# A graph-attention and mixture-FFN kernel: the square of a pair's second tile of updated rows moves from the end of ScalarE's slot to its beginning

## The reference: what is computed

```
xn    = layernorm(x)                       # before: x + attention
Wh    = xn @ W.T ; e = leaky_relu(ei[:,None] + ej[None,:], 0.2)
alpha = softmax(where(adj == 0, -inf, e))  # 1024 x 1024 per graph
x1    = x + alpha @ Wh                     # "updated rows"
feat  = mean over the 16 graphs of layernorm(x1) ; w = softmax(feat @ Wr + br)
out   = x1 + sum over 8 experts of w * (three-layer FFN of layernorm(x1))
```

## Time and profile before

| | |
|---|---|
| median of 3 runs | 2808.72 us (2807.88 to 2809.81) |
| time of the profiled execution | 2809.31 us |
| its span in the profile | 2807.4 us |
| PE busy / PEld busy | 2774.5 us (99%) / 2469.6 us (88%) |
| DVE busy / ACT busy / POOL busy | 2413.1 (86%) / 2106.8 (75%) / 487.5 us (17%) |
| attention part | about 0 to 683 us, 128 slots |
| granted TensorE clock | 0.998 of full speed |

### The profile page before, as it was taken

One profiled execution on the slowest core, in us unless ns is written; L12 is line 12 of the kernel. 1 busy time (PEld: TensorE's weight loads), 2 busy tenths in 40 slices (PEclk: granted clock), 3 DMA queues, 4 the chain that ended last, 5 costly groups with the idle time before them and its releaser, 6 DMA issues.

```text
span 2807.4 us, 46140 instructions
## 1 busy us (share of the span) xinstructions
PE 2774.5 (99%) x17114; PEld 2469.6 (88%) x17114; DVE 2413.1 (86%) x3408; ACT 2106.8 (75%) x2832; POOL 487.5 (17%) x707
## 2 busy tenths in 40 slices
PE   8999999999999999999999999999999999999998
PEld 7999999998788888888888888888888888888887
DVE  8999999997888888888888888888888888888887
ACT  7889889887777777777777777777777777777775
POOL 4555555555000000000000000000000000001000
PEclk9999999999999999999999999999999999999999
DMA  4455555543455554545445455545545554545554
GB/s 163 154 167 163 157 166 162 162 153 119 139 170 165 161 166 154 165 156 161 163 155 165 154 165 161 165 153 170 157 163 157 160 164 154 166 154 163 153 162 145
DMA packets 160060, 445.91 MB, mean 159 GB/s; under 512 B 16032, under 2 KB 73800, under 8 KB 159840
## 3 DMA queue, kind: packets, MB, share of 16 engines
q1 hardware_dynamic: 159840, 442.98, 50.2%
HBM read 401.99 MB, written 40.93 MB: 158 GB/s over the span
## 4 chain that ended last, share of the span: by engine, by line
PE 74%; DVE 1%; ACT 0%; issue 0%; DMA 0%; DVEq 0%; ACTq 0%
PE head_ps L53 12%; PE head_ps L55 12%; PE head_ps L54 12%; PE m_ps L1284 7%; PE m_ps L1287 7%; PE m_ps L1286 7%; PE z_ps L55 4%; PE z_ps L53 4%; PE z_ps L54 4%; PE turn_ps L1257 1%; PE turn_ps L1265 1%; DVE h_lo L1569 0%; DVE h_sums L1576 0%; DMA wo_ops<-wo_scratch 0%; ACT h_hi L1432 0%
## 5 line engine op out<-in xcount | busy, mean ns | idle before, releaser
L1416 ACT ACTIVATE h<-head_ps,bn_shift,bn_scale 128x512 f32<-128x512 f32 x768 | 593.9, 774 | 532.5 <-PE head_ps L55 319.9
L1569 DVE TENSOR_TENSOR h_lo<-h_sums,h_hi 128x1792 fp32r<-128x1792 f32 (+1 forms) x257 | 518.2, 2017 | 199.9 <-ACT h_hi L1432 199.8
L1432 ACT ACTIVATE h_hi<-h_sums 128x1792 fp32r<-128x1792 f32 (+1 forms) x257 | 435.4, 1694 | 63.6 <-DVE h_sums L1589 58.0
L1576 DVE TENSOR_TENSOR h_sums<-h,gate_row 128x1024 f32<-128x1024 f32 x256 | 313.7, 1225 | 114.5 <-ACT h L1416 96.7
L87 POOL TENSOR_TENSOR ffn_vareps<-ffn_mv,ln_eps 128x4 f32<-128x4 f32 x32 | 7.1, 223 | 1860.4 <-DVE ffn_mv L81 1860.4
L1536 DVE TENSOR_TENSOR h_lo<-h,h_hi 128x1024 fp32r<-128x1024 f32 x256 | 311.9, 1218 | 6.8 <-ACT h_hi L1446 6.8
L53 PE MATMUL attn_ps<-wh_hi,pT_hi 128*128 128x256 f32 x1024 | 304.9, 298 | 0.0
L54 PE MATMUL attn_ps<-wh_lo,pT_hi 128*128 128x256 f32 x1024 | 287.9, 281 | 0.0
L55 PE MATMUL attn_ps<-wh_hi,pT_lo 128*128 128x256 f32 x1024 | 287.8, 281 | 0.0
L1446 ACT ACTIVATE h_hi<-h 128x1024 fp32r<-128x1024 f32 x256 | 270.9, 1058 | 0.1
L1284 PE MATMUL m_ps<-h_hi,wo_ops 128*128 128x256 f32 x896 | 256.0, 286 | 3.1 <-DMA wo_ops<-wo_scratch 3.1
(11 more groups left out here) (215 smaller groups left out, 7619.3 us busy)
## 6 DMA issues: line engine op xcount, KB each, us to landing
wh_lo<-wo_scratch SPq DMA_DIRECT2D x124, 896.0 KB, 6.4
wo_ops<-wo_scratch SPq DMA_DIRECT2D x124, 896.0 KB, 6.5
adj_sb<-in_adj SPq DMA_DIRECT2D x128, 512.0 KB, 3.5
gate_row<-w_scratch SPq DMA_DIRECT2D x256, 256.0 KB, 4.6
x_sb<-in_x SPq DMA_DIRECT2D x64, 256.0 KB, 2.9
x_scratch<-x_sb SPq DMA_DIRECT2D x128, 128.0 KB, 1.8
ffn_x<-x_scratch SPq DMA_DIRECT2D x16, 512.0 KB, 7.6
x_sb<-x_scratch SPq DMA_DIRECT2D x16, 512.0 KB, 7.5
```

The lines of the kernel that those rows point to most:

```text
L1416: return act.activation(dst, src, ACT.Relu, bias=bn_shift[layer][:, col], scale=bn_scale[layer][:, col])
L1432: act.activation(h2_hi[s % 2][:, a:b, :], g2[:, 1 + a:1 + b, :], ACT.Copy) \
L1569: dve.tensor_tensor(h2_lo[s % 2][:, a:b, :], g2[:, 1 + a:1 + b, :], bits(h2_hi[s % 2][:, a:b, :]), ALU.subtract).then_inc(S["h2_lo_ready"], 1)
L1576: dve.tensor_tensor(h2_rows, h2[:, :, :], gate[s % 2][:, :].unsqueeze(1).to_broadcast([P, KB, BANK]), ALU.mult).then_inc(S["gated_ready"], 1)
```

## The change

The square of the second tile of a pair is issued as the first instruction of ScalarE's odd slot, ahead of the copies, the relu and `pT_hi`, and no longer just ahead of the exponentials. The square of the first tile, in the even slot, stays where it is. The last two slots of the last pair of graphs keep their own order. The instruction, its tiles and its semaphores are the same.

```diff
+            def square(pt, pn, step):
+                at = (pt + step) % 4
+                act.wait_ge(S["x1_negmean_ready"], pn)
+                act.activation(w_sb[:, at % 2, :], x1_sb[at][:, :], ACT.Square, bias=x1_negmean[:, at:at + 1],
+                               accum_out=x1_squares[:, at:at + 1]).then_inc(S["x1_squares_ready"], 1)
+
             def slot(k, u, last):
                 head = head_at(k, u, last)
+                post, pt, pn, _ = pair_at(k, u, 0, last)
+                if post and not (last and u == UT - 1):
+                    square(pt, pn, 0)
...
-                squares = [pair_at(k, u, 1, last) + (-1,), pair_at(k, u, 0, last) + (0,)]
+                squares = [pair_at(k, u, 1, last) + (-1,)]
                 if last and u == UT - 2:
-                    squares[1] = pair_at(k, u + 1, 0, last) + (0,)
+                    squares.append(pair_at(k, u + 1, 0, last) + (0,))
                 if last and u == UT - 1:
                     squares = []
                 for post, pt, pn, _, step in squares:
                     if post:
-                        at = (pt + step) % 4
-                        act.wait_ge(S["x1_negmean_ready"], pn)
-                        act.activation(w_sb[:, at % 2, :], x1_sb[at][:, :], ACT.Square, bias=x1_negmean[:, at:at + 1],
-                                       accum_out=x1_squares[:, at:at + 1]).then_inc(S["x1_squares_ready"], 1)
+                        square(pt, pn, step)
```

## The result

The changed kernel takes 2827.15 us (median; 2826.81 to 2828.1 in 3 runs) against 2808.72 before: a ratio of 1.0068, 95% interval 1.0054 to 1.0082. It is slower by 18.4 us; 2827.7 was forecast. The profiled execution has a span of 2825.2 us, 17.8 more than before.

What follows compares the result with a forecast made beforehand. VectorE (slots 2 to 7), then TensorE, were taken to pace each block; 14 blocks at 1.41 us, less 0.7 in the tail, gave +19.0 on the profiled 2809.31, less 0.6 to the median: 2827.7 us, range 2809 to 2831.

Steps and rivals of the forecast that it cites:

- What bounds the kernel: Attention blocks of eight slots: VectorE sets the pace from slot 2 to slot 7, TensorE from there to slot 2.
- Slots 7, 1 and 5, the square itself: Moved square costs nothing: hidden by ScalarE's wait for TensorE in slots 7 and 1, by VectorE's work in slot 5.
- Slot 3: ScalarE's `pT_hi` ends later, so VectorE's `pT_lo` starts late: 0.39 us lost per block on the path.
- the signs: Expected in the profile: `pT_lo` waiting about 0.5 us in slot 3, L973 at 2.25 us in slot 7, 42.1 us blocks.
- the gain of slot 2: VectorE's L973 in slot 2 becomes free of GpSimd, 0.18 us less, swallowed by the wait for `pT_hi` in slot 3.
- Slot 7: GpSimd's L541 starts 0.10 us ahead of VectorE's L973, which then takes 2.25 us, 1.05 more, on the path.
- Rival 1: Slot 7: VectorE's L973 gets the port and L541 waits; +4.3 us, 2813.0; chance 0.26.
- rival 2: Mixed slot 7s: L541 wins in about half, 2820 us; chance 0.08.
- The sum: Per block 0.39 - 0.03 + 1.05 = 1.41 us, 14 blocks 19.7 us; less 0.7 in the tail, +19.0.
- the tail: Last pair's slots 3 to 15, paced by ScalarE: 0.7 us taken back, between 0 and 2.
- Rivals 3 to 5: Earlier exponentials pay, around 2800 (0.07); move does nothing, 2806 to 2811 (0.09); slots 7/1 copy late, a few us.

Runs made afterwards that it cites:

- front in slots 3 alone: Kernel before, with the square moved first in ScalarE's slot only in slots 3 of the first seven pairs: 2813.98 us, ratio 1.0018.
- the padded kernel: Changed kernel plus one small GpSimd addition ahead of L541 in slots 7 of the first seven pairs: 2810.74 us, ratio 1.0007.
- front in slots 7 alone: Kernel before, with the square moved first in ScalarE's slot only in slots 7 of the first seven pairs: 2823.63 us, ratio 1.0053.
- front in slots 1 and 5 alone: Kernel before, with the square moved first only in slots 1 and 5 of the first seven pairs: 2809.4 us, ratio 1.0003.

## Why the prediction was right

*What bounds the kernel.* Right. The extra reduction on VectorE costs time in slot 3 and none in slot 1, and each loss in slots 3 and 7 came out as a longer block and a longer wait of L638.

*Slots 7, 1 and 5, the square itself.* Right: no loss in slots 1 and 5, and with L541 held back none in slot 7 (blocks of 40.61 to 40.70 us when slot 3 is left out too).

*Slot 3.* Forecast 0.36 us net per block; with only this loss left the blocks are 0.3 us longer (front in slots 3 alone, or the padded kernel). In the changed kernel `pT_lo` of slot 3 (398.80) starts 6.44 us behind `ej_rows` of slot 2 (392.36), before (388.59) 6.06 us behind it (382.53): 0.38 us lost, 0.39 forecast. It waits only 0.34 us for `pT_hi`, not the 0.5 named among the signs, for I had let VectorE come 0.16 us earlier by the gain of slot 2. All but 0.05 us of that was swallowed, and already in slot 2, not by the wait in slot 3 as the prediction has it.

*Slot 7.* Forecast: L541 0.10 us ahead, masking 2.25 us, 1.05 more. Measured: 0.08 to 0.10 ahead, 2.28 to 2.30, 14 times of 14. Rival 1 (VectorE wins) and rival 2 (mixed) fall. The padded kernel shows both the mechanism and how near rival 1 was: 0.15 us later on GpSimd comes near its 2813.0 (2810.7). The rule of the Trainium skill (SBUF — State Buffer, "Who interferes with whom"), that the first to issue holds the pair, gave the right winner in slot 7: ahead by 0.08 to 0.10 us GpSimd won, 14 times. The power in slot 3 does not fit it (last section).

*The sum.* From the second on, a block is 1.40 us longer (42.1 against 40.7), and 1.41 was forecast: this part is right in its terms. The nearness of the total, 0.6 us, is partly luck, for two other terms were off, and both the same way. The first of the 14 blocks grew by only 0.45 us (42.53 to 42.98), where I had counted it in full. Slot 3's loss does not count there: front in slots 3 alone leaves this block at 42.16 us, and kernels that have the old order in it take 42.19 to 42.53, while front in slots 7 alone makes it 43.31. TensorE waits there for `wh_lo` in slot 6 too, as the timeline of the kernel before shows for its weight loads, but that this is the reason was not tried.

```profile
77.23 0.42 PEld L638 LDWEIGHTS head_ps<-ident,x_sb 128*128 128x128 f32 x4 [0.85 <-DVE wh_lo L925]
```

And the tail gave back 2.2 us, where I took 0.7 between 0 and 2: that term was mis-sized. That ScalarE paces the tail, as the prediction has it, no run here shows. The two terms together make the loss some 2.5 us smaller than forecast. The total still came out near, because the rest of the FFN part is 1.4 us longer in the profile, which I had put at nothing, and because I had taken off 0.6 us for the step from profile to median, while the changed kernel was profiled at its median. The FFN stretch varies from 2123.5 to 2126.4 us across the profiles of these kernels with the same code, and what makes it vary stays open.

*Rivals 3 to 5.* The earlier exponentials released nobody: TensorE's wait for them is 12.0 us against 12.7. The move was not neutral, and the copy in slots 7 and 1 was not late to any cost.

## What to carry to other kernels

An instruction that is moved, even to a place where it costs nothing itself, also moves whatever it releases. Here the square fitted into a pause of its own engine, but it let GpSimd's chain in slot 7 start 3.3 us earlier (1.13 us ahead of the masking, not 2.15 behind it), onto the VectorE instruction that it shuts out. So follow the released chain to its end and lay it beside the instructions of the engine that it can shut out. When the order of arrival hangs on 0.1 us, fix it in the code: here a wait of GpSimd for the masking cost nothing that could be told and took the chance out.

## What the runs showed of the hardware

- Which of GpSimd and VectorE goes first was decided by less than 0.15 us, and the same way 14 times of 14 on either side: ahead by 0.08 to 0.10 us GpSimd wins and VectorE's 1.20 us become 2.28; behind by 0.06 it loses and its own 1.28 us become 2.32. The loser waits for the end of the other's instruction, and then still takes nearly its own time: 1.09 us after it for the masking, 1.18 for the addition.
- When an instruction of GpSimd that follows another at once asks within some 0.05 us of VectorE's, the outcome varies within one execution. The 0.05 is an estimate from L570, whose second half starts about 0.55 us behind its first, and the masking of slot 4, which starts 0.54 to 0.60 behind it in 12 of the 14 blocks of the kernel before. That masking took 1.20 to 1.28 us in 11 of these and 1.63 in one; with front in slots 1 and 5 alone it took 1.64 in two blocks and 1.21 to 1.30 in eleven.
- GpSimd's power -0.5 (L563) had started 0.07 to 0.08 us ahead of the masking in slot 3 in 13 of the 14 blocks of the changed kernel, and the masking still took 1.22 us, as without it: this power did not shut VectorE out as the addition and the scaling of rows did. The other way round it was shut out: a power that starts 0.10 us behind the masking of slot 6 (L533 at 401.31) takes 1.67 us and not 0.69. The timeline of the changed kernel in slot 3, and the masking of slot 6 in the kernel before:

```profile
397.17 0.70 POOL L563 TENSOR_TENSOR x_rstd<-x_vareps,minus_half 128x2 f32<-128x2 f32 x1
397.24 1.22 DVE L980 SCALAR_TENSOR_TENSOR scores<-adj_sb,ej_rows 128x1024 f32<-128x1024 int32 x1
```

```profile
401.21 1.20 DVE L973 SCALAR_TENSOR_TENSOR scores<-adj_sb,ej_rows 128x1024 f32<-128x1024 int32 x1
```
